# Attention values in one group of matmuls per key block instead of two half groups

## The chip, the cores and the metric

The kernel runs on one core of a Trainium2 chip. The metric is the device time of one execution in microseconds; the kernel before has a median of 934.62 us in three runs.

## The reference

Two transformer layers on 2048 tokens of width 128. The change touches the first layer's attention alone, which has 8 heads, 2 query and key dimensions and 16 value dimensions a head, over all 2048 keys:

```python
q = (x @ Wq.T + bq).reshape(B, M, H, dqk)      # dqk = 2
k = (x @ Wk.T + bk).reshape(B, M, H, dqk)
v = (x @ Wv.T + bv).reshape(B, M, H, dv)       # dv = 16
scores = einsum('bmhd,bnhd->bhmn', q, k) / sqrt(dqk)
scores = where(scores >= 0, scores, 0.2 * scores)
beta = softmax(scores, axis=-1)
out = gamma * einsum('bhmn,bnhd->bmhd', beta, v) + x
...
```

Around it stand a mixture of 64 experts with 6 chosen, a lookup attention and a mixture of 8 experts with 2 chosen, each behind a layer norm. They are the same in both kernels.

## The kernel before

The attention stage works in 8 rounds: 4 chunks of 512 queries (`c`) times 2 groups of 4 heads (`g`). A round goes over 16 key blocks of 128 keys (`n`), and a key block is two pairs (`hp` 0 and 1), a pair being two heads. So there are 256 pairs, numbered `u`, 32 in a round; an even `u` is the first pair of its key block, an odd one the second. The keys lie on the partitions of the scores and the queries in the columns.

A pair goes through these steps, each on 128 partitions by 2 x 512 columns:
- `scores(u)` on PE (line 575): two bf16 products, side by side in the array, into two banks of PSUM. There are three such buffers of two banks, used in turn, so scores(u) waits until exp(u-3) has read them (`exp_done`).
- relu, `max(4 s, 0)` in place, on DVE (line 1474). In the rounds with the routing work (below), slots 14, 25, 27 and 31 are on ACT instead (line 1011).
- `shifted(u)` on PE (line 588): two bf16 products that add the scores once more, less a bound per query, onto the same banks. It waits for the relu.
- exp on ACT (line 1015) into a float32 buffer `PB` in SBUF, which holds a whole key block. There are three, and exp of a block's first pair waits until the values of three blocks ago are done (`values_done`).
- `values(u)` on PE (line 603): the exps times the values `VS`, 32 columns a head (16 values, a one for the sum, zeros). The four heads of the group have a quarter of the array's columns each, and add up over the 16 key blocks in one bank of PSUM, 6 or 7 by the round. A float32 product shows as two records in the trace. Each group covers all four heads and half of the queries, so it needs both exps of its block.

PE's order is written out by hand: for each u, shifted(u), then scores(u+2), then values(u-2). After the fifth exp of a round ACT copies the sums of the round before out of PSUM (line 994). In the three rounds with c >= 1 and g = 0, the norm and the router of the chunk before are done in between: PE's parts stand behind the values of slots 6, 9 (line 617), 18 (626), 21 (633) and 28 (642 to 648) of the 32, DVE's behind slots 8, 11, 13, 24, 26 and 30. The scatter of the chunk's rows by POOL (line 1197) is paced by counts of exps; that of the last chunk follows the stage.

Of the kernel before, what the change touches and what calls it, by code (L numbers as in the profile page):

```python
# [14 lines left out]
NT = T // P  # L15
BANK = 512
CH = 512
# [4 lines left out]
HG = H // G  # L22
# [101 lines left out]
def build(nc, a, out):  # L124
# [12 lines left out]
    with ctx:  # L137
        def sb(name, shape, dt=f32, stack=ctx):
            return stack.enter_context(nc.sbuf_tensor(name, shape, dt))
# [3 lines left out]
        def sem(name):  # L143
            if name not in sems:
                sems[name] = ctx.enter_context(nc.semaphore(name))
            return sems[name]
# [36 lines left out]
        PS = ctx.enter_context(nc.psum_tensor("PS", [P, 8 * BANK], f32))  # L183
# [5 lines left out]
        def cb(name, lo=0, hi=None):  # L189
            s, e = BC[name]  # L190
            return CB[:, s + lo:(s + hi if hi else e)]

        def pf(name):
            s, e = PFC[name]
            return PF[:, s:e]
# [34 lines left out]
        PB = [sb(f"PB{i}", [P, HG, CH], f32, att) for i in range(3)]  # L230
# [3 lines left out]
        VS = sb("VS", [P, NT, H, 32], f32, att)  # L234
# [85 lines left out]
        def pair_of(u):  # L320

            rnd, r = divmod(u, PER_ROUND)
            c, g = ROUNDS[rnd]
            return rnd, c, g, r // 2, r % 2
# [141 lines left out]
        def _(pe):  # L466
            mm = nc.tensor.matmul
# [68 lines left out]
            for g in range(G):  # L536
                mm(PS[:, g * P:(g + 1) * P], hxy[:, g, 0, :], pf("vx"), start=True, stop=False)
                last = mm(PS[:, g * P:(g + 1) * P], hxy[:, g, 1, :], pf("vy"), start=False, stop=True)
# [6 lines left out]
            for i in range(4):  # L545
                if i >= 2:
                    pe.wait_ge(sem("bound_ready"), i - 1)
                for t in range(4 * i, 4 * i + 4):
                    for g in range(G):
                        at = 2 * (i % 2) * BANK + (2 * (t % 4) + g) * P  # L550
                        last = mm(PS[:, at:at + P], QS[g][:, t * P:(t + 1) * P], VV[:, g * P:(g + 1) * P], start=True, stop=True)
# [8 lines left out]
            for g in range(G):  # L560
                for t in range(NT):
                    last = mm(PS[:, 4 * g * BANK + t * P:4 * g * BANK + (t + 1) * P], MR[:, g, t, :], cb("identb"), start=(g == 0),
                              stop=True, skip_group_check=True)
# [27 lines left out]

            def values(u):

                rnd, c, g, n, part = pair_of(u)
                if n == 0 and part == 0 and rnd >= 2:
                    pe.wait_ge(sem("sums_taken"), rnd - 1)
                    if g == 1:
                        pe.wait_ge(sem("counts0_out"), c)
                pe.wait_ge(sem("exp_done"), u - part + 2)
                q = slice(part * CH // 2, (part + 1) * CH // 2)  # L600
                at = (6 + rnd % 2) * BANK
                for j in range(HG):
                    last = mm(PS[32 * j:32 * j + 32, at + q.start:at + q.stop], VS[:, n, g * HG + j, :],  # L603
                              PB[u // 2 % 3][:, 2 * (j % 2) + j // 2, q], start=(n == 0 and part == 0), stop=(n == NT - 1),
                              skip_group_check=True)
                last.then_inc(sem("values_done"), 1)

            def sums_turned(q, part, b):

# [44 lines left out]
            for u in range(N_PAIRS):  # L654
                shifted(u)
                if u + 2 < N_PAIRS:
                    scores(u + 2)
                if u >= 2:
                    values(u - 2)
                rnd, c, g, n, hp = pair_of(u)  # L660
                r = u % PER_ROUND
                if c >= 1 and g == 0:
                    if r == 6:
                        sums_turned(c - 1, 0, 7)
                    if r == 9:
                        sums_turned(c - 1, 1, 7)
                    if r == 18:
                        rows_turned(c - 1, 7)
                    if r == 21:
                        gates0(c - 1, 7)  # L670
                    if r == 28:
                        counts0(c - 1, 7)
            values(N_PAIRS - 2)
            values(N_PAIRS - 1)

            pe.wait_ge(sem("counts0_out"), NC - 1)
# [33 lines left out]
            for k in range(2):  # L710
                for h in range(2):
                    last = mm(PS[0:1, 2 * BANK + (2 * k + h) * P:2 * BANK + (2 * k + h + 1) * P], tcol[:, k, h:h + 1], ident,
                              start=True, stop=True)
# [1155 lines left out]
```

## Time and profile before

| | |
|---|---|
| median of 3 runs | 934.62 us (931.69 to 935.87) |
| the profiled execution | 936.18 us, of which span 934.4 us |
| PE busy | 715.6 us, 77% of the span |
| DVE busy | 630.0 us, 67% |
| ACT busy | 449.1 us, 48% |
| mean granted clock of TensorE | 0.863 |

Busy times are shares of the whole span, which has many stages. The attention stage runs from about 52 to 382 us. PE here is TensorE's matmul, PEld its weight loads, DVE VectorE, ACT ScalarE, POOL GpSimd, SP SyncE. In the groups, "L603" is line 603. The ends of matmuls are modelled, so their starts are the better measure. In the chain a step counts up to the start of the next one, so the records of a group overlap less there than in the timeline.

### The profile page before, as it was taken

Reading aid. Unit: us, or ns where it says so; the run is one execution under the profiler, and the core shown is the slowest. Engines: PE = TensorE matmul, PEld = TensorE weight load, DVE = VectorE, ACT = ScalarE, POOL = GpSimd, SP = SyncE. Lnnn points to the kernel's source line nnn. Section 1 sums busy time; section 2 is a strip of 40 time slices with the busy share of each in tenths; the row PEclk is TensorE's granted clock in tenths of the full one; section 3 lists DMA queues with packets and bytes.
Section 4 is the critical chain, followed back from the end, with each engine's and each line's share of the span. In section 5 each row is a group of like instructions: output and inputs, shape, how many; then the busy total and the mean of one; then the engine's idle time right before and its main releaser. Section 6 shows DMA issues by size and latency. Waiting matters only on the chain.

```text
span 934.4 us, 17256 instructions
## 1 busy us (share of the span) xinstructions
PE 715.6 (77%) x5879; PEld 424.4 (45%) x5880; DVE 630.0 (67%) x1367; ACT 449.1 (48%) x605; POOL 432.6 (46%) x671
## 2 busy tenths in 40 slices
PE   4789999999999999538898998016264653699992
PEld 2332223223222222214898998013223422699992
DVE  7879998999899999373576754246767454244442
ACT  3668887888888888301343444001101011365550
POOL 5010002362254235455676775677657552255552
PEclk9879999999999999869899999556575556799997
DMA  4499999999999901512697665112111110143336
GB/s 156 144 270 276 302 282 312 362 290 298 288 303 314 297 22 44 127 51 75 179 259 221 166 172 146 45 50 52 51 45 49 44 43 24 37 51 48 48 49 149
DMA packets 83334, 143.45 MB, mean 154 GB/s; under 512 B 10720, under 2 KB 75584, under 8 KB 81744
## 3 DMA queue, kind: packets, MB, share of 16 engines
q1 hardware_dynamic: 57600, 118.07, 43.5%
q0 software_dynamic: 12784, 17.40, 8.3%
q10 hardware_dynamic: 12864, 6.89, 2.6%
q8 instruction: 48, 0.79, 0.4%
q14 instruction: 38, 0.31, 0.1%
HBM read 117.13 MB, written 101.34 MB: 234 GB/s over the span
## 4 chain that ended last, share of the span: by engine, by line
PE 59%; DVE 12%; POOL 8%; DMA 7%; issue 6%; ACT 6%; SPq 2%; POOLq 0%; DVEq 0%
PE PS L603 13%; PE PS L588 7%; PE PS L575 7%; PE PS L907 6%; ACT PB L1015 3%; PE PS L751 3%; POOL GB L1239 3%; DMA XP<-slots_scratch 3%; PE PS L917 3%; PE PS L738 3%; PE PS L740 3%; POOL slots_scratch L1197 2%; PE PS L726 2%; PE PS L855 1%; DMA sums_scratch<-YO,XG 1%
## 5 line engine op out<-in xcount | busy, mean ns | idle before, releaser
L1474 DVE TENSOR_SCALAR PS<-PS 128x1024 f32<-128x1024 f32 x244 | 289.7, 1227 | 15.5 <-PE PS L575 11.6
L1015 ACT ACTIVATE PB<-PS 128x1024 f32<-128x1024 f32 x256 | 260.5, 1025 | 54.3 <-PE PS L588 46.6
L603 PE MATMUL PS<-PB,VS 128*32 128x256 f32 x2048 | 164.2, 393 | 0.6 <-ACT PB L1015 0.5
L1197 POOL DMA_INDIRECT slots_scratch<-XN,slot x96 | 93.6, 975 | 59.8 <-ACT PB L1015 39.0
L1239 POOL DMA_INDIRECT GB<-y_scratch,slotc x96 | 91.7, 955 | 37.0 <-issue 28.6
L575 PE MATMUL PS<-QS,KP 64*128 64x512 bf16 x512 | 99.3, 385 | 10.7 <-ACT PB L1015 6.0
L588 PE MATMUL PS<-QM,KP 64*128 64x512 bf16 x512 | 100.7, 390 | 1.3 <-DVE PS L1474 1.2
L1282 POOL DMA_INDIRECT sums_scratch<-YO,XG x39 | 60.8, 1558 | 61.9 <-DVE YO L1797 58.8
L907 PE MATMUL PS<-XTT,WB 128*128 128x128 f32 x624 | 78.4, 281 | 0.0
L907 PEld LDWEIGHTS PS<-XTT,WB 128*128 128x128 f32 x624 | 75.0, 197 | 0.3 <-issue 0.3
L588 PEld LDWEIGHTS PS<-QM,KP 64*128 64x128 bf16 x512 | 24.6, 93 | 104.3 <-issue 50.4
L603 PEld LDWEIGHTS PS<-PB,VS 128*32 128x32 f32 x2048 | 40.5, 108 | 65.6 <-issue 64.1
L1074 ACT COPY XT<-PS 128x512 f32<-128x512 f32 x8 | 4.7, 585 | 122.9 <-PE PS L775 122.9
L1223 POOL COPY WQ<-W0GU 128x192 f32 x160 | 55.3, 346 | 14.8 <-issue 10.4
L1207 POOL TENSOR_TENSOR X<-X,TQ 128x256 f32<-128x256 f32 x8 | 5.8, 724 | 121.3 <-DVE TQ L1425 121.3
L775 PE MATMUL PS<-CF,XN 128*128 128x128 f32 x32 | 8.9, 434 | 68.8 <-DVE XN L1617 68.8
L1790 DVE COPY XTT<-PS 128x128 f32<-128x128 f32 x39 | 11.4, 291 | 70.8 <-PE PS L895 70.8
L1604 DVE SCALAR_TENSOR_TENSOR X<-GB,wtok,X 128x128 f32<-128x128 f32 x96 | 33.7, 352 | 31.2 <-DMA GB<-y_scratch,slotc 28.4
L575 PEld LDWEIGHTS PS<-QS,KP 64*128 64x128 bf16 x512 | 24.5, 93 | 60.5 <-ACT PB L1015 47.8
L1063 ACT ACTIVATE SP<-PS 96x256 f32<-96x256 f32 x80 | 30.4, 380 | 45.0 <-PE PS L740 44.8
L1116 ACT COPY WB<-W1GU 128x1024 f32 x39 | 40.7, 1046 | 22.7 <-PE PS L907 15.0
L1040 ACT COPY YP<-PS 128x256 f32<-128x256 f32 x80 | 29.8, 372 | 40.1 <-PE PS L751 39.9
(281 smaller groups left out, 1298.5 us busy)
## 6 DMA issues: line engine op xcount, KB each, us to landing
y_scratch<-YP SPq DMA_DIRECT2D x80, 128.0 KB, 2.5
slots_scratch<-slots_scratch SPq DMA_DIRECT2D x1, 8768.0 KB, 37.1
W0GU<-in_w0gu SPq DMA_DIRECT2D x1, 6144.0 KB, 124.3
XP<-slots_scratch ACTq DMA_DIRECT2D x80, 64.0 KB, 2.7
XP<-slots_scratch SPq DMA_DIRECT2D x80, 64.0 KB, 2.7
W1GU<-in_w1gu SPq DMA_DIRECT2D x8, 512.0 KB, 4.3
W0D<-in_w0d SPq DMA_DIRECT2D x1, 3072.0 KB, 16.7
XG<-slots_scratch SPq DMA_DIRECT2D x39, 68.5 KB, 2.2
```

Source lines behind the costliest of these rows:

```text
L575: last = mm(bank(2 * (u % 3) + k), KP[g][hp][r, n * P:(n + 1) * P], QS[g][r, c * CH:(c + 1) * CH], start=True, stop=True)
L588: last = mm(bank(2 * (u % 3) + k), KP[g][hp][r, n * P:(n + 1) * P], QM[g][r, c * CH:(c + 1) * CH], start=False, stop=True, skip_group_chec ...
L603: last = mm(PS[32 * j:32 * j + 32, at + q.start:at + q.stop], VS[:, n, g * HG + j, :], PB[u // 2 % 3][:, 2 * (j % 2) + j // 2, q], start=( ...
L907: last = mm(PS[:, at + k * P:at + (k + 1) * P], WB[j % 2][:, w], XTT[j % 2][:, :], start=True, stop=True)
L1015: A(PB[u // 2 % 3][:, 2 * hp:2 * hp + 2, :], pair_banks(u).rearrange("p (j q) -> p j q", j=2), ACT.Exp).then_inc(sem("exp_done"), 1)
L1116: nc.scalar.copy(WB[j % 2][:, :], W1GU[:, ds(expert, 1), :].squeeze(1)).then_inc(sem("w_placed"), 1)
L1197: gp.indirect_dma_start(slots0_dram.rearrange("b p d -> (b p) d"), bass.IndirectOffsetOnAxis(ap=slot0[:, t, k:k + 1], axis=0), XN[:, t, 0: ...
L1223: gp.tensor_copy(WQ[j % 6][:, :], W0GU[:, ds(expert, 1), :].squeeze(1)).then_inc(sem("wq_ready"), 1)
L1239: gp.indirect_dma_start(GB[:, t, k, :], None, y0_dram.rearrange("b p d -> (b p) d"), bass.IndirectOffsetOnAxis(ap=slotc[:, t, k:k + 1], ax ...
L1282: gp.indirect_dma_start(sums_dram[j % 2][:, :], bass.IndirectOffsetOnAxis(ap=XG[j % NXG][:, P:P + 1].bitcast(i32), axis=0), YO[j % 4][:, : ...
L1474: TS_(pair_banks(u), pair_banks(u), 4.0, 0.0, ALU.mult, ALU.max).then_inc(sem("relu_done"), 1)
L1604: step(STT(X[:, t, :], GB[:, t, k, :], wtok[:, t, k:k + 1], X[:, t, :], ALU.mult, ALU.add))
```

## The change

The values products of a key block run once, for all 512 queries, behind the second pair (odd u) of the block in PE's order; behind the first pair nothing is left. The count `values_done` goes up by 2 there instead of by 1 twice. Types, operands and the accumulation over key blocks stay.

```diff
--- before.py
+++ after.py
@@ -591,19 +591,18 @@
 
             def values(u):
 
-                rnd, c, g, n, part = pair_of(u)
-                if n == 0 and part == 0 and rnd >= 2:
+                rnd, c, g, n, hp = pair_of(u)
+                if hp == 0:
+                    return
+                if n == 0 and rnd >= 2:
                     pe.wait_ge(sem("sums_taken"), rnd - 1)
                     if g == 1:
                         pe.wait_ge(sem("counts0_out"), c)
-                pe.wait_ge(sem("exp_done"), u - part + 2)
-                q = slice(part * CH // 2, (part + 1) * CH // 2)
-                at = (6 + rnd % 2) * BANK
+                pe.wait_ge(sem("exp_done"), u + 1)
                 for j in range(HG):
-                    last = mm(PS[32 * j:32 * j + 32, at + q.start:at + q.stop], VS[:, n, g * HG + j, :],
-                              PB[u // 2 % 3][:, 2 * (j % 2) + j // 2, q], start=(n == 0 and part == 0), stop=(n == NT - 1),
-                              skip_group_check=True)
-                last.then_inc(sem("values_done"), 1)
+                    last = mm(PS[32 * j:32 * j + 32, (6 + rnd % 2) * BANK:(7 + rnd % 2) * BANK], VS[:, n, g * HG + j, :],
+                              PB[u // 2 % 3][:, 2 * (j % 2) + j // 2, :], start=(n == 0), stop=(n == NT - 1), skip_group_check=True)
+                last.then_inc(sem("values_done"), 2)
 
             def sums_turned(q, part, b):
```

## Rows read from the trace of the kernel before

**Rows 1.** The page: busy times, and the span in 40 slices of 23.4 us.

```profile
PE 715.6 (77%) x5879; PEld 424.4 (45%) x5880; DVE 630.0 (67%) x1367; ACT 449.1 (48%) x605; POOL 432.6 (46%) x671
...
PE   4789999999999999538898998016264653699992
...
DVE  7879998999899999373576754246767454244442
...
PEclk9879999999999999869899999556575556799997
DMA  4499999999999901512697665112111110143336
```

**Rows 2.** The page: costliest groups (busy us, mean ns | idle before, releaser).

```profile
L1474 DVE TENSOR_SCALAR PS<-PS 128x1024 f32<-128x1024 f32 x244 | 289.7, 1227 | 15.5 <-PE PS L575 11.6
L1015 ACT ACTIVATE PB<-PS 128x1024 f32<-128x1024 f32 x256 | 260.5, 1025 | 54.3 <-PE PS L588 46.6
L603 PE MATMUL PS<-PB,VS 128*32 128x256 f32 x2048 | 164.2, 393 | 0.6 <-ACT PB L1015 0.5
...
L575 PE MATMUL PS<-QS,KP 64*128 64x512 bf16 x512 | 99.3, 385 | 10.7 <-ACT PB L1015 6.0
L588 PE MATMUL PS<-QM,KP 64*128 64x512 bf16 x512 | 100.7, 390 | 1.3 <-DVE PS L1474 1.2
```

**Rows 3.** Timeline of ACT, copies of the sums: start us, us.

```profile
100.18 0.58 ACT L994 COPY OT<-PS 128x512 f32<-128x512 f32 x1
...
138.72 0.58 ACT L994 COPY OT<-PS 128x512 f32<-128x512 f32 x1
...
182.96 0.58 ACT L994 COPY OT<-PS 128x512 f32<-128x512 f32 x1
```

**Rows 4.** The chain in a plain stretch: start us, us, what.

```profile
120.96 0.39 PE PS L575 x2
121.34 0.57 PE PS L603 x8
121.91 0.32 PE PS L588 x2
122.24 0.22 PE PS L575 x2
122.45 0.57 PE PS L603 x8
123.02 0.32 PE PS L588 x2
```

**Rows 5.** Timeline of PE, same stretch.

```profile
120.96 0.39 PE L575 MATMUL PS<-QS,KP 64*128 64x512 bf16 x2
121.28 0.64 PE L603 MATMUL PS<-PB,VS 128*32 128x256 f32 x8
121.85 0.39 PE L588 MATMUL PS<-QM,KP 64*128 64x512 bf16 x2
122.07 0.38 PE L575 MATMUL PS<-QS,KP 64*128 64x512 bf16 x2
...
123.36 0.39 PE L575 MATMUL PS<-QS,KP 64*128 64x512 bf16 x2
```

**Rows 6.** Timeline of ACT, same stretch.

```profile
120.98 1.02 ACT L1015 ACTIVATE PB<-PS 128x1024 f32<-128x1024 f32 x1
122.28 1.02 ACT L1015 ACTIVATE PB<-PS 128x1024 f32<-128x1024 f32 x1 [0.27 <-PE PS L588]
```

**Rows 7.** Timeline of DVE, three relus that start one after the other.

```profile
120.13 2.49 DVE L1474 TENSOR_SCALAR PS<-PS 128x1024 f32<-128x1024 f32 x2
...
121.39 1.23 DVE L1474 TENSOR_SCALAR PS<-PS 128x1024 f32<-128x1024 f32 x1
...
122.53 1.22 DVE L1474 TENSOR_SCALAR PS<-PS 128x1024 f32<-128x1024 f32 x1
```

**Rows 8.** Windows of 2.40 us and lulls: busy by engine, granted clock.

```profile
core 0: us, PE busy (x) PEld busy (x) DVE busy (x) ACT busy (x) POOL busy (x), PEclk, DMA share, GB/s
...
119.98:122.38 2.40, 2.39 (x26) 0.69 (x24) 2.36 (x3) 2.04 (x3) 0.00 (x0) 1.00 0.48 137
...
164.00:170.00 6.00, 5.13 (x50) 1.32 (x48) 5.83 (x19) 6.00 (x9) 0.72 (x1) 1.00 1.04 445
460.00:467.00 7.00, 4.27 (x24) 4.27 (x25) 2.03 (x6) 1.25 (x4) 1.57 (x7) 0.76 0.62 156
500.00:511.00 11.00, 8.85 (x67) 8.63 (x66) 5.69 (x15) 3.38 (x9) 5.66 (x19) 0.84 0.72 201
```

**Rows 9.** The values line: ns min, median, max.

```profile
L603 PE MATMUL PS<-PB,VS x2048: 378/403/634, 57.5 to 381.7; 128*32 128x256 f32 x187
```

**Rows 10.** Line 695, float32 records of 512 columns; its timeline.

```profile
L695 PE MATMUL PS<-XT,wshg x32: 591/592/1169, 412.4 to 436.9; 128*96 128x512 f32 x32
...
421.24 3.60 PE L695 MATMUL PS<-XT,wshg 128*96 128x512 f32 x8
```

**Rows 11.** The chain in a mixed round: routing pieces on PE.

```profile
141.24 0.59 PE PS L617 x4
...
157.39 0.59 PE PS L626 x4
...
161.78 1.03 PE PS L633 x8
...
172.13 0.21 PE PS L642
172.34 0.17 PE PS L645 x3
172.51 0.11 PE PS L648
```

**Rows 12.** The chain at the stage's end.

```profile
380.99 1.11 PE PS L603 x16
```

**Rows 13.** Timeline of PE at the lower clock.

```profile
56.93 0.61 PE L575 MATMUL PS<-QS,KP 64*128 64x512 bf16 x2
57.47 1.08 PE L603 MATMUL PS<-PB,VS 128*32 128x256 f32 x8
58.48 0.61 PE L588 MATMUL PS<-QM,KP 64*128 64x512 bf16 x2
```

## Prediction

> **What bounds the kernel now.** I read the page first, for its busy times and its forty slices. PE, DVE and ACT are all busy through the first dense stretch, and PE and DVE both read as full there [rows 1]. That stretch is the attention stage, and the three costliest lines of the kernel lie in it [rows 2]. A busy share near 100% on two engines doesn't say which one sets the pace, so I went on to the order of time.
>
> The copies of the finished sums stand at the same place in every round and so mark the rounds [rows 3]. A round without the routing work (plain) takes 100.18 to 138.72, or 38.54 us for 32 pairs: 1.20 us a pair. A round with it (mixed) takes 138.72 to 182.96, or 44.24 us. There are five plain rounds and three mixed ones.
>
> The chain of a plain stretch is PE alone, in a pattern that repeats after two pairs and 2.40 us [rows 4]. But the chain hides that two of its steps only just made it. The timeline shows this [rows 5, 6]. With the starts there:
> - exp (ACT) of a pair starts at 120.98, takes 1.02, ends at 122.00, and the scores that need its banks run from 122.07. In the other half of the pattern it is 122.28 + 1.02 = 123.30, and the scores start at 123.36: they waited for exp.
> - From those scores to the values products behind them: 120.96 to 121.28, 0.32 us.
> - From the values products to the shifted scores behind them: 121.28 to 121.85, 0.57 us.
> - From the shifted scores to the exp that they release: 121.85 to 122.28, 0.43 us, and the exp takes 1.02 + 0.06 to the next scores.
>
> These make a closed loop: exp(u-1), scores(u+2), values(u-2), shifted(u+1), exp(u+1). The scores wait for exp because there are three buffers of pair banks, and PE works in program order. Its length is 1.02 + 0.06 + 0.32 + 0.57 + 0.43 = 2.40 us for two pairs, exactly the measured pattern. DVE is next: its starts are 120.13, 121.39, 122.53 [rows 7], so 1.26 us apart where it waits for scores and 1.14 where it has work. DVE alone could do two pairs in 2.28. ACT does its two in 2.04 [rows 8].
>
> **The change, part by part.** Removed: per key block, eight matmul records (four products, two records each) of 256 columns, and their eight weight loads. Added: the remaining eight have 512 columns. Moved: all of a block's values work stands behind the odd pair; behind the even pair there is nothing. No DMA is moved.
>
> *The length of the wide group.* A 256-column record takes 378 ns at the least (median 403) [rows 9]. The trace has no products of 32 stationary columns by 512, but it has float32 records of 512 columns, and those take 591 ns at the least and follow each other every (3.60 - 0.59) / 7 = 0.43 us [rows 10]. So 512 columns cost 0.213 us more in each of the two passes of a group; the four heads run side by side in both cases. Group: 0.57 + 2 x 0.213 = 1.00 us. Lower bound: the passes alone, 2 x 0.43 = 0.86. Upper bound: nothing saved over two narrow groups, 1.14. I take 1.00, since the same chip clock and the same type stand in the row.
>
> A page of the Trainium skill, TensorEngine Tiling (Array Packing), section Instruction Overhead, says that each matmul carries about 60 cycles of overhead. By it, as an estimate, dropping eight records in two pairs would save 8 x 25 ns = 0.20 us of the 1.14, and the group would be 0.94 us; the loop below would be 2.77 us instead of 2.83, some 8 us less in all. No row here separates the overhead of a record, since four run at once.
>
> *What it frees.* PE work in two pairs falls from 2 x 0.57 to 1.00, so by 0.14 us. That is worth something only if PE's total work is the limit.
>
> *What it lengthens.* The loop through the odd pair now holds the wide group: 1.02 + 0.06 + 0.32 + 1.00 + 0.43 = 2.83 us for two pairs. The loop through the even pair has no values group: about 1.02 + 0.06 + 0.22 + 0.43 = 1.73 (0.22 is scores right behind shifted [rows 4]). A loop can't be averaged with the other, since each comes round once in two pairs, and the longer one sets the pace. So a plain pair goes from 1.20 to 1.415 us, +0.213. Followed in time from an exp of an even pair at 0: the next exp, whose shifted scores were ready long before, runs 1.02 to 2.04; the scores wait until 1.08; the wide group runs 1.40 to 2.40; the shifted scores of the next even pair, whose relu was ready, only then start, and its exp at 2.83. DVE has relus for 2.28 of each 2.83 and waits; ACT for 2.04.
>
> *The waits.* values(u-2) needs the exps of its whole block, that is up to u-2. At that point PE has already waited for exp(u-1) in the scores ahead of it, so no new wait arises. The buffers of exp's output are freed at the same slot as before for the odd pair, and exp of three blocks later is behind shifted scores that stand behind that group; no wait there. The sums of a round are complete at the same slot.
>
> *Mixed rounds.* A mixed round costs 44.24 - 38.54 = 5.7 us over a plain one. PE's inserted work is 0.59 + 0.59 + 0.59 + 1.03 + 0.21 + 0.17 + 0.11 = 3.29 us [rows 11] (the piece of line 617 comes twice and stands there once); the rest, 2.4, is ACT and DVE work, among it four relus on ACT. After the change the pieces behind even pairs (slots 6, 18, 28) fall into the short loop, which has 2.83 - 1.73 = 1.1 us to spare, and cost nothing. Slots 9 and 21 are odd and add 0.59 + 1.03 = 1.62 to the long loop. Of the 2.4 on ACT and DVE, something between all and none remains, since ACT's spare time in two pairs grows from 0.36 to 0.79. Surcharge: 1.6 to 4.0, I take 2.8. A mixed round becomes 32 x 1.415 + 2.8 = 48.1 us, +3.8.
>
> *Behind the stage.* The work after the last exp is a chain of its own [rows 12]: it shortens by about 0.1 (two narrow groups, 1.11, become one of 1.00). POOL's scatters inside the stage wait for counts of exps and stretch with it; its last 24 come after. The background transfers end before the stage does [rows 1] and gain slack.
>
> **Sum.** Five plain rounds x 32 x 0.213 = 34.1, less about 0.6 because the first pairs run at the start-up and the last ones drain: 33.5. Three mixed rounds x 3.8 = 11.4. Together +45. The profiled execution took 936.2 us (span 934.4 and 1.8 around it), 1.6 above the median of the three runs shown. 936.2 + 45 - 1.6 = 979.6; I say 979 us, 4.8% slower.
>
> **The rivals.**
> - *The pace follows PE's total work (same or a little better).* If the two loops were averaged, or the buffers gave enough slack, two pairs would need DVE's 2.28. Then plain pairs gain 0.06 us, 160 x 0.06 = 9.6 us, and mixed ones perhaps half: 921 to 926 us. For it: DVE is 98% busy [rows 8], and in the average over two pairs every engine has room. Against it: the loop of five measured steps gives the measured 2.40 to the last digit, and none of its waits is loosened by the change. With enough slack in the buffers to absorb just the lump but no more, it would be 935.
> - *The wide group costs no more than a narrow one (faster, the other side).* If a group's 0.57 were a price per instruction and not per column, V = 0.57, PE would be free for longer and the loop would stay at 2.40; mixed rounds would get up to 2 us shorter each: about 929. It decides at V = 0.57: every 0.01 above costs 0.005 x 256 = 1.3 us. Against it: [rows 9, 10], 378 against 591 ns.
> - *The clock.* PE now has holes of up to 0.7 us in 2.83 us. The granted clock fell where PE sat idle for microseconds at a stretch, to a mean of 0.76 and 0.84, and stayed at 1.00 in the lull of a mixed round [rows 8]. At the lower level (1.2 GHz) a narrow group takes 57.47 to 58.48, 1.01 us, scores to values 0.54, shifted scores 0.61 [rows 13]. The loop would be 1.08 + 0.54 + (1.01 + 0.85) + 0.66 = 4.14, +0.65 us a pair on top; with a fifth of the stage at that level, 979 + 33 = 1012.
> - *The group is dearer than two narrow ones make it look* (V = 1.14): loop 2.97, 1.485 a pair. Plain 160 x 0.285 = 45.6, mixed 3 x 6.1 = 18: 998 us. With V = 0.86: loop 2.69, plain 160 x 0.145 = 23.2, mixed 3 x 1.6 = 4.8: 962.
>
> **How the numbers follow.** Forecast (slower by the long loop, group of 0.86 to 1.14): 0.87. Clock on top of it: 0.04. Pace by total work: 0.06, of which half within 0.5% of before. Group at the narrow price: 0.03. A measurement of this kernel tells about 0.5% from no change, 4.7 us. Slower 0.91, same 0.03, faster 0.06. The range comes from the group's length, mostly between 0.88 and 1.10, and the mixed surcharge between 1.6 and 5.7 us (-3.6 to +8.7 in all): 964 to 993. It leaves out the clock and both faster rivals.
>
> **What would show it.** In the profile after, 1024 records of L603 (its new line) with 512 columns near 0.59 us; the chain of a plain stretch as exp, scores, values 1.00, shifted, with exp pairs every 2.83 us; rounds near 45.3 and 48 us between the copies; ACT and DVE with their busy times unchanged and their idle time before exp and relu grown by some 40 us, released by PE; a granted clock of 1.00. A group near 0.57, or rounds of 38 us, would make the prediction wrong; so would rounds of 45 with a gap elsewhere given back, of which I see none.

## The result and the profile after

The changed kernel takes 972.34 us (971.05 to 974.88, 4 runs) against 933.62 us for the one before in the same session: ratio 1.042, interval 1.038 to 1.045. It is slower by 39 us. (The profile after has one source line fewer, so that exp is line 1014 and relu 1473.) The profiled execution took 974.88 us, 38.7 more than that of before (936.18). The forecast was 979 us, range 964 to 993.

The page of the profile after, its busy times and slices; it answers to [rows 1]:

```profile
PE 682.4 (70%) x4855; PEld 392.8 (40%) x4856; DVE 639.9 (66%) x1367; ACT 440.0 (45%) x605; POOL 432.3 (44%) x671
...
PE   4777777877877787744888999403653654499992
...
DVE  7788888888888889837366774236677564144442
...
PEclk9889999999999999986999999855756557699996
```

PE has 1024 records fewer and 33 us less to do, and the stage is longer. In its slices PE reads 7 where it read 9, DVE 8 where it read 9, and the granted clock reads 9 from the fourth slice on until the stage ends, as it did before. No engine is full any more, which points to waits and not to work. The costliest groups answer to [rows 2]:

```profile
L1473 DVE TENSOR_SCALAR PS<-PS 128x1024 f32<-128x1024 f32 x244 | 299.1, 1232 | 45.4 <-PE PS L575 38.1
L1014 ACT ACTIVATE PB<-PS 128x1024 f32<-128x1024 f32 x256 | 250.7, 1022 | 104.6 <-PE PS L588 103.9
L575 PE MATMUL PS<-QS,KP 64*128 64x512 bf16 x512 | 99.3, 385 | 78.8 <-ACT PB L1014 76.1
L603 PE MATMUL PS<-PB,VS 128*32 128x512 f32 x1024 | 137.1, 608 | 0.6 <-ACT PB L1014 0.6
```

The idle time before exp went from 54.3 to 104.6 us and ends with the shifted scores; that before relu from 15.5 to 45.4, ended by the scores; that before the scores from 10.7 to 78.8, ended by exp. These three waits point at each other in a ring. The chain in a plain stretch shows the ring, and answers to [rows 4]:

```profile
131.28 1.03 ACT PB L1014
132.32 0.05 issue
132.36 0.39 PE PS L575 x2
132.75 0.99 PE PS L603 x8
133.75 0.34 PE PS L588 x2
134.09 0.02 issue
134.11 1.03 ACT PB L1014
```

exp at 131.28, scores at 132.36, wide values group, shifted scores, exp at 134.11: 2.83 us for two pairs, to the last digit of the forecast. The timeline of PE gives the starts, and answers to [rows 5]:

```profile
132.36 0.39 PE L575 MATMUL PS<-QS,KP 64*128 64x512 bf16 x2 [0.69 <-ACT PB L1014]
132.68 1.06 PE L603 MATMUL PS<-PB,VS 128*32 128x512 f32 x8
133.68 0.39 PE L588 MATMUL PS<-QM,KP 64*128 64x512 bf16 x2
```

132.68 to 133.68 is the group: 1.00 us. Ahead of it PE sits idle for 0.69 us, waiting for exp; behind it everything waits for PE. The copies of the sums answer to [rows 3]:

```profile
106.75 0.58 ACT L993 COPY OT<-PS 128x512 f32<-128x512 f32 x1
...
152.00 0.58 ACT L993 COPY OT<-PS 128x512 f32<-128x512 f32 x1
...
199.16 0.58 ACT L993 COPY OT<-PS 128x512 f32<-128x512 f32 x1
```

A plain round takes 152.00 - 106.75 = 45.25 us (38.54 before), a mixed one 47.16 (44.24 before). The stage ends, by its last copy, at 422.9 us instead of 382.1: +40.8. Some 2 us come back behind it: the stage of the 64 experts (first to last turned pair) took 133.1 instead of 136.2 us, in single executions.

### The profile page after: what moved, and what is told of

The parts are those of the page before. It is cut to its first block, busy times and chain, and to the rows that moved or that the text cites. A ratio compares the mean times of both kernels' runs of the same rounds, so it can differ in the third digit from the quotient of the medians.

```text
span 973.1 us, 15208 instructions
## 1 busy us (share of the span) xinstructions
PE 682.4 (70%) x4855; PEld 392.8 (40%) x4856; DVE 639.9 (66%) x1367; ACT 440.0 (45%) x605; POOL 432.3 (44%) x671
## 4 chain that ended last, share of the span: by engine, by line
PE 52%; ACT 16%; DVE 13%; DMA 7%; POOL 6%; issue 5%; SPq 2%; POOLq 0%; DVEq 0%
ACT PB L1014 13%; PE PS L603 12%; PE PS L906 7%; PE PS L575 5%; PE PS L588 4%; DMA XP<-slots_scratch 4%; PE PS L916 3%; POOL GB L1238 3%; PE PS L750 3%; PE PS L737 2%; PE PS L739 2%; PE PS L725 1%; PE PS L854 1%; ACT PS L1010 1%; DMA sums_scratch<-YO,XG 1%
## 5 line engine op out<-in xcount | busy, mean ns | idle before, releaser
L1473 DVE TENSOR_SCALAR PS<-PS 128x1024 f32<-128x1024 f32 x244 | 299.1, 1232 | 45.4 <-PE PS L575 38.1
L1014 ACT ACTIVATE PB<-PS 128x1024 f32<-128x1024 f32 x256 | 250.7, 1022 | 104.6 <-PE PS L588 103.9
L575 PE MATMUL PS<-QS,KP 64*128 64x512 bf16 x512 | 99.3, 385 | 78.8 <-ACT PB L1014 76.1
L603 PE MATMUL PS<-PB,VS 128*32 128x512 f32 x1024 | 137.1, 608 | 0.6 <-ACT PB L1014 0.6
L1549 DVE COPY XQ<-PS 128x256 f32<-128x256 f32 x54 | 22.9, 425 | 33.3 <-PE PS L725 33.3
```

The costliest lines, as they stand in the source:

```text
L575: last = mm(bank(2 * (u % 3) + k), KP[g][hp][r, n * P:(n + 1) * P], QS[g][r, c * CH:(c + 1) * CH], start=True, stop=True)
L603: last = mm(PS[32 * j:32 * j + 32, (6 + rnd % 2) * BANK:(7 + rnd % 2) * BANK], VS[:, n, g * HG + j, :], PB[u // 2 % 3][:, 2 * (j % 2) + j ...
L1014: A(PB[u // 2 % 3][:, 2 * hp:2 * hp + 2, :], pair_banks(u).rearrange("p (j q) -> p j q", j=2), ACT.Exp).then_inc(sem("exp_done"), 1)
L1473: TS_(pair_banks(u), pair_banks(u), 4.0, 0.0, ALU.mult, ALU.max).then_inc(sem("relu_done"), 1)
```

## The experiments

The experiments ran on three chips: the first four on one, the repeats and the two bf16 kernels on a second, and the other four, in a single execution each, on a third. On the first two of these chips the stages behind attention were 53 to 59 us longer, for every kernel profiled there, than in the first profile of the kernel before, which itself took 1016 and 1003 us there. So the totals that were expected in us can't be compared with the measured ones. I read ratios, and above all the rounds inside the stage, which no later stage touches: 45.25 us for the changed kernel in its first profile and again on the second chip.

**Two narrow groups together.** Is it the wide product, or the place of the work?

```diff
-                for j in range(HG):
-                    last = mm(PS[... whole bank ...], VS[:, n, g * HG + j, :], PB[...][:, 2 * (j % 2) + j // 2, :], ...)
+                for part in range(2):
+                    q = slice(part * CH // 2, (part + 1) * CH // 2)
+                    for j in range(HG):
+                        last = mm(PS[... half bank q ...], VS[:, n, g * HG + j, :], PB[...][:, 2 * (j % 2) + j // 2, q], ...)
```

> The changed kernel, but the block's values products are two narrow groups (256 queries each) one right after the other behind the odd pair, instead of one wide group. Theory (the loop exp, scores, values, shifted, exp through the odd pair sets the pace, with the length of all the values work that stands in it): the lump is 1.11 to 1.14 us instead of 1.00, two pairs take 2.94 to 2.97 us instead of 2.83, a plain round 47.0 to 47.5 us, the kernel 986 to 990 us, though PE's total work is just that of the kernel before. Rival (the wide product itself is what costs, not the place): two narrow groups are as before, 2.40 us for two pairs and about 934 us.

Ratio 1.022 to the kernel before on its chip (interval 1.017 to 1.027, so it is slower, though not clearly by 2%), and a plain round of 152.76 - 107.43 = 45.33 us in the first of them. Its chain:

```profile
120.67 1.03 ACT PB L1018
121.70 0.05 issue
121.75 0.39 PE PS L575 x2
122.14 1.00 PE PS L606 x16
123.14 0.34 PE PS L588 x2
123.48 0.02 issue
123.51 1.03 ACT PB L1018
```

It is the place: narrow products in the lump are as slow as wide ones, with 2.84 us for two pairs, though PE issues exactly the records of the kernel before. The size was expected too long: 16 narrow records take 1.00 us, not 1.11 to 1.14. So a second narrow group right behind the first adds only 0.43 us, and of a lone group's 0.57 us, 0.14 is paid once for the whole run of values products, however many records it has. The ratio is smaller than the rounds make one expect: no profile of the kernel before was taken on this chip, but on the second one its attention stage was itself longer, as told below.

**Half the queries, and three quarters.** Does the lump's length set the pace even when PE has far less to do?

```diff
-                    last = mm(PS[32 * j:32 * j + 32, (6 + rnd % 2) * BANK:(7 + rnd % 2) * BANK], VS[:, n, g * HG + j, :],
-                              PB[u // 2 % 3][:, 2 * (j % 2) + j // 2, :], ...)
+                    w = CH if n == 0 else CH // 2          # 384 and 32 in the two others
+                    last = mm(PS[32 * j:32 * j + 32, at:at + w], VS[:, n, g * HG + j, :],
+                              PB[u // 2 % 3][:, 2 * (j % 2) + j // 2, 0:w], ...)
```

> The changed kernel, with the values products of key blocks 1 to 15 of a round only for the first 256 queries (the other half of these products is left out), behind the odd pair. Theory: the group is as long as a narrow one, 0.57 us, so the long loop is 1.83 + 0.57 = 2.40 us for two pairs, the same as in the kernel before, although half of the values work is gone and nothing stands behind the even pairs; plain rounds near 38.6 us, mixed ones some 41 to 42, in all about 920 to 926 us. Rival (the pace follows an engine's total work, DVE's 1.14 us a pair being the next): 2.28 us for two pairs, plain rounds near 36.6 us, about 912 us.

> The changed kernel, with the values products of key blocks 1 to 15 only for the first 384 queries (a quarter of these products is left out). Theory: the group takes 1.00 - 2 x 0.107 = 0.79 us, the long loop 2.62 us for two pairs, a plain round 41.9 us: on the line between 38.85 (256 queries) and 45.25 (512). Rival (the pace has steps, or follows total work): anything off that line.

Copies of the sums with half the queries, then with 384:

```profile
98.47 0.58 ACT L995 COPY OT<-PS 128x512 f32<-128x512 f32 x1
...
137.33 0.58 ACT L995 COPY OT<-PS 128x512 f32<-128x512 f32 x1
```

```profile
102.31 0.58 ACT L995 COPY OT<-PS 128x512 f32<-128x512 f32 x1
...
144.36 0.58 ACT L995 COPY OT<-PS 128x512 f32<-128x512 f32 x1
```

Plain rounds of 38.86 and 42.05 us. With half of the values work left out, a plain round is no shorter than in the kernel before (38.54), as the loop of 1.83 + 0.57 = 2.40 says and total work denies. The first key block of a round keeps its full group, so the round is 15 x 2.40 + 2.83 = 38.83 us. The three points 256, 384 and 512 queries lie on a line, 38.86, 42.05 and 45.25: 3.2 us a step over the 15 shortened blocks, or 0.213 us a block for each 128 queries, which is the forecast's price of streaming. The mixed round with half the queries took 42.9 us, more than the 41 to 42 expected. Its ratio is 0.974 (0.969 to 0.979), more of a gain than its stage shows (last copy at 376.7 us, 382.1 in the first profile of the kernel before); some of that may be the late exps told below, but the kernel before was not profiled on this chip. The one run with 384 took 957.7 us beside 936.6.

**Nearly no values.**

> The changed kernel, with the values products of key blocks 1 to 15 only for 32 queries (nearly all of these products are left out). Theory: the group takes some 0.2 us, the long loop 2.05 us, below DVE's two relus of 2.28 us, so the line ends there: a plain round 36.3 to 36.8 us as in the bf16 kernels, not the 33 us that the loop alone would give. Rival (PE alone sets the pace in float32): below 36 us.

Windows of that kernel, the plain rounds 1, 3 and 5 (the columns are those of [rows 8]):

```profile
95.10:132.30 37.20, 28.91 (x256) 8.68 (x256) 36.76 (x33) 32.89 (x34) 0.00 (x0) 0.95 0.99 283
...
178.30:216.60 38.30, 31.98 (x256) 9.00 (x256) 37.70 (x33) 32.85 (x35) 19.14 (x20) 0.82 1.00 296
261.60:298.50 36.90, 28.03 (x256) 8.57 (x256) 36.53 (x33) 32.93 (x34) 19.13 (x20) 1.00 0.98 299
```

A partial miss: 36.9 us at full clock, 37.2 and 38.3 where the granted clock fell to its lower level for part of the round. DVE is busy for 36.5 of 36.9 us, so the line does end at DVE. The whole took 931.3 us beside 936.6. What I hadn't counted on is that the granted clock falls inside the stage when PE has this little left to do. In the changed kernel it did not.

**Values ahead of the scores.** The same wide group, moved out of the loop of exp.

```diff
                 shifted(u)
-                if u + 2 < N_PAIRS:
-                    scores(u + 2)
                 if u >= 2:
                     values(u - 2)
+                if u + 2 < N_PAIRS:
+                    scores(u + 2)
```

> The changed kernel, with PE's order shifted(u), values(u-2), scores(u+2) instead of shifted, scores, values. Theory: the wide group leaves the loop of exp (which becomes 1.73 us) but enters the one of relu: relu 1.23, to shifted 0.05, to values 0.32, to scores 1.00, to relu 0.44, which is 3.04 us for two pairs instead of 2.83; plain rounds near 48.6 us and the kernel near 995 to 1000 us. Rival (only the loop through exp counts, or PE's hole before the scores swallows the group): 2.28 to 2.4 us for two pairs and the kernel at or below the kernel before, 915 to 935 us.

Ratio 1.043 (1.038 to 1.048). Its chain has DVE where ACT was:

```profile
120.07 1.24 DVE PS L1473
...
121.36 0.39 PE PS L588 x2
121.75 0.99 PE PS L603 x8
122.75 0.34 PE PS L575 x2
...
123.11 1.24 DVE PS L1473
```

3.04 us for two pairs and a plain round of 157.69 - 109.05 = 48.64 us, both as expected. The hole of 0.69 us ahead of the scores can't be filled this way: the group then delays the scores, and through them relu. Both rings run through PE, and in both of the places tried one of them holds the lump.

**The routing pieces on even slots.**

```diff
-                    if r == 9:
+                    if r == 10:
                         sums_turned(c - 1, 1, 7)
...
-                    if r == 21:
+                    if r == 22:
                         gates0(c - 1, 7)
```

> The changed kernel, with the two routing pieces of PE that stand behind wide groups (slots 9 and 21, 0.59 and 1.03 us) moved one slot on, to 10 and 22, where no values group stands. Theory: there they lie in the short loop, which has 1.1 us to spare, and a mixed round (47.15 us, 1.9 over a plain one) loses up to 1.6 us: 45.5 to 46.2 us, the kernel 3 to 5 us faster than the changed one. Rival (the surcharge is ACT's and DVE's work, or the later release of ACT makes it good): mixed rounds stay at 47 us and the time doesn't move.

The mixed round between its copies went from 47.16 to 198.30 - 152.01 = 46.29 us, just outside the range expected: 0.87 us of the 1.62. The stage ends at 420.35 us, 2.6 earlier. Its ratio on the chip of the first four is 1.016 (1.013 to 1.020); that session has no run of the changed kernel to set it against. Its chain at slot 10 shows what takes the place:

```profile
159.75 0.60 PE PS L616 x4
160.35 0.02 issue
160.38 0.27 DVE og L1423
160.65 0.02 issue
160.67 0.48 DVE TQ L1424
161.15 1.15 DVE PS L1473
```

PE had room for the piece there, but DVE waits for its result right behind slot 11, and now stands waiting with the next relu behind it. This leaves 0.37 us. At slot 22 it is ACT that reads the piece's result (line 1003) ahead of a relu and the next exps, and 0.61 us are left. I had counted PE's room and not the distance to the reader.

**Products in one pass.** The group shortened with nothing left out: exp's output and the values are rounded to bf16.

```diff
-        PB = [sb(f"PB{i}", [P, HG, CH], f32, att) for i in range(3)]
+        PB = [sb(f"PB{i}", [P, HG, CH], bf16, att) for i in range(3)]
...
-        VS = sb("VS", [P, NT, H, 32], f32, att)
+        VS = sb("VS", [P, NT, H, 32], bf16, att)
```

> The changed kernel, with exp's output and the values in bf16 instead of float32 (the sums are still added in float32), so that a product is one pass and not two. Theory: the wide group takes 0.21 + 0.14 = 0.35 us, the long loop 2.18 us, which is below DVE's two relus of 2.28, so DVE sets the pace: plain rounds near 36.6 us, mixed ones 41 to 42, and the kernel faster than the one before by some 18 to 22 us in the stage. Lumping costs nothing once the group is under 0.45 us. Rival (the order of PE costs 0.2 us a pair whatever the length): plain rounds of 40 us or more.

> The kernel before (two narrow groups), with exp's output and the values in bf16. Theory: narrow group 0.25 us, loops 2.08 us, DVE sets the pace at 2.28: the same stage time as the wide bf16 kernel within 1 us a round. Rival (fewer, wider instructions help once PE is not in the loop): the wide one is faster by its 0.14 us a key block, 2 us a round.

Copies of the sums, wide and then narrow:

```profile
94.49 0.58 ACT L993 COPY OT<-PS 128x512 f32<-128x512 f32 x1
...
130.80 0.58 ACT L993 COPY OT<-PS 128x512 f32<-128x512 f32 x1
```

```profile
96.31 0.58 ACT L994 COPY OT<-PS 128x512 f32<-128x512 f32 x1
...
132.62 0.58 ACT L994 COPY OT<-PS 128x512 f32<-128x512 f32 x1
```

Both plain rounds take 36.31 us: by the sum, a group under 2.28 - 1.83 = 0.45 us leaves the bound to DVE, and lumping is free. Where nothing held the products behind a group, the wide one took 0.33 us and the narrow one 0.22, start to start. A wide one:

```profile
58.57 0.39 PE L575 MATMUL PS<-QS,KP 64*128 64x512 bf16 x2 [0.41 <-ACT PB L1014]
58.89 0.40 PE L603 MATMUL PS<-PB,VS 128*32 128x512 bf16 x4
59.22 0.39 PE L588 MATMUL PS<-QM,KP 64*128 64x512 bf16 x2
```

The difference, 0.11 us, is 256 columns, so 512 columns stream in 0.21 us, a quarter of the 0.86 in float32 (half as many records, each half as long). 0.12 us is left over in either group, though every product around it is bf16 too. So most of the 0.14 us of the float32 group is not the price of a change of type. The products also change their shape in the array there, from 64x128 to 128x32 and back; no run separates that from other causes.

Against the kernel before, the wide one has a ratio of 0.969 (0.966 to 0.972), the narrow one 0.975 (0.973 to 0.977). Both beat both kernels of this study. Of the 7 us between the two medians, 3.9 lie in the stage of the profiled executions. There the later plain rounds, in which scatters run, are 36.7 and 36.5 us in the wide one against 38.0 and 37.9 in the narrow one, more than the 1 us a round that was expected. In each of those rounds of the narrow one a single exp starts 1.3 to 1.4 us late, with ACT free and the shifted scores there (at 178.32 and 258.07 us), which is as much as the two kernels differ; so it is not the groups that cost the time. Two of three mixed rounds go the other way by 0.9 us (42.7 in the wide one, outside the 41 to 42 expected); at the end of both, the wide one's granted clock fell to the lower level (238.8 to 242.2 and 317.3 to 324.1 us).

**The two kernels again, on the second chip.**

> The kernel before, unchanged, as a control for this chip, whose stages behind attention ran some 50 us longer in the first four experiments. Expected: plain rounds 38.54 us and mixed ones 44.25 us, as in the first profile, a ratio of 1, and the extra time in the stages behind attention. If the rounds differ here, the experiments have to be read against them.

> The changed kernel, unchanged, on the same chip. Expected: plain rounds 45.25 us and mixed ones 47.15 us, the last copy of the sums 40.8 us later than in the kernel before. If the ratio is again 1.042 the loss is the stage's; if it is nearer 1.02, as the first four experiments suggest, some 20 us are given back in the stages behind it on this chip, and the two traces show where.

Ratio of the first 1.001 (0.998 to 1.003), of the changed kernel 1.028 (1.025 to 1.031). The difference to 1.042 does not lie behind the stage, as was expected, but in the stage, and in the kernel before. Its round 3, which in the first profile took 38.54 us:

```profile
183.75 0.58 ACT L994 COPY OT<-PS 128x512 f32<-128x512 f32 x1
...
224.69 0.58 ACT L994 COPY OT<-PS 128x512 f32<-128x512 f32 x1
```

40.94 us here, and rounds 5 and 7 grew too, so that its stage ends at 395.2 instead of 382.1. The changed kernel's rounds are 45.25 and 47.15 on this chip as well, and its stage ends at 422.6. Its loss in the stage is thus 27.4 us here and 40.8 there. The timeline of ACT and PE in that round shows a late exp:

```profile
204.34 2.16 ACT L1015 ACTIVATE PB<-PS 128x1024 f32<-128x1024 f32 x2 [0.28 <-issue]
...
206.31 0.39 PE L588 MATMUL PS<-QM,KP 64*128 64x512 bf16 x2
...
207.44 1.94 ACT L1015 ACTIVATE PB<-PS 128x1024 f32<-128x1024 f32 x2 [0.94 <-PE PS L588]
```

ACT is free at 206.50 and the shifted scores of 206.31 release exp 0.43 us later, at 206.74 as everywhere else; it starts at 207.44, 0.7 us late. In rounds 5 and 7 this comes about every fourth pair. Over the three rounds the late starts add up to some 13 us, as much as the stage is longer.

**What makes exp late?**

```diff
                 chunk_norm(q)
                 chunk_route(q)
+            for q in range(NC):
                 chunk_scatter(q)
```

> The kernel before, unchanged, as the control of this call: plain rounds 38.54 us where no scatters run, and either 38.5 or 39 to 43 us in the plain rounds with scatters, by the chip.

> The kernel before, with POOL's 72 scatters of the first three chunks moved behind the attention stage. It is for the late starts of exp (0.7 us every fourth pair) that the kernel before showed in the rounds with scatters on the second chip. If the scatters' transfers cause them, all plain rounds here are 38.54 us, also where the control of this call has more; if not, they stay long. The whole gets some 90 us longer in any case (72 scatters at 1.26 us).

Inconclusive. This chip behaved as the first one: in one execution the control took 936.8 us with all plain rounds at 38.54, and so did the kernel with the scatters behind the stage (1025.1 us in all). With nothing to remove, the run says nothing on the cause.

## Why the prediction was right

- *What bounds the kernel.* Right: the loop exp, scores, values, shifted, exp. The group's length moves the pace by just its own length (256, 384, 512 queries), the same records in another place cost the same as the wide ones, and where the group leaves this loop it enters the one of relu with the length worked out for it.
- *The wide group.* 1.00 us forecast, 1.00 measured. The upper bound of 1.14 counted twice what is paid once: two narrow groups in a row take 1.00 too. By the rule of about 60 cycles for each matmul (the Trainium skill, TensorEngine Tiling (Array Packing), Instruction Overhead), read as a cost that every record adds, the wide group would have been shorter than two narrow ones in a row by eight records' worth, 0.20 us as an estimate; the trace doesn't agree: 45.25 against 45.33 us a round is 0.005 us a key block. Why the extra records cost nothing, no run shows.
- *Plain rounds.* +6.8 us forecast, +6.71 measured.
- *Mixed rounds.* The term that was mis-sized: a surcharge of 2.8 us (1.6 to 4.0), where 1.90 was measured, so +2.9 a round instead of +3.8, and 2.7 us in all. The two pieces behind wide groups cost their full 1.62 us, as they stand in the chain with the whole of their length:

```profile
159.20 0.59 PE PS L616 x4
...
176.76 1.03 PE PS L632 x8
```

From exp to exp, those two steps are 0.58 and 1.04 us over 2.83, and the pieces behind even pairs cost nothing, as forecast. Of the 2.4 us of ACT and DVE work only 0.28 remains, where 1.2 was taken. That ACT's longer waits take in the rest is likely but was not tested by itself.
- *Sum.* The stage grew by 40.8 us, not 45: 2.7 of the difference is the mixed rounds; 1.4 is the plain ones, of which the first and the last grew less than I took (6.6 up to the first copy, 5.4 behind the seventh, 3 x 6.71 between). The 0.1 us saved at the end did not come: the last group takes 1.11 up to the copy of the sums, as the two before it did.
- *Behind the stage.* Nothing was forecast to come back; 2.1 us did in the profiled pair of executions. Its cause was not looked for. The forecast of 979 us was 7 too high; 4.2 of that is the stage and 2.1 this.
- *The rivals.* Total work as the pace is refuted by the kernel with half the queries; the price per instruction by 1.00 against 0.57; the granted clock was 1.00 from 60 us to the end of the stage, in both kernels. It fell inside the stage with 32 queries and, for 3 to 7 us at a time, in both bf16 kernels.

What stays open is why the kernel before loses 13 us in the stage on the second chip, through exps that start 0.7 us late in the rounds with scatters, and why the changed kernel shows none of it. That a late start hides in ACT's idle time, 0.8 us ahead of each two exps, is only argued, and the kernel with two narrow groups together speaks against it: it has the same idle time, and its rounds 3 and 5 grew to 46.3 and 46.5 us all the same, with two exps each 0.5 to 0.6 us late. Late exps showed only in three kernels, all with two narrow groups a key block (the one before on the second chip, the one with both groups together, the narrow bf16 one); the kernel with half the queries, with one narrow group a block, ran on the same chip as the second of them and had none. They make the changed kernel's loss 28 us instead of 39 there, with the same sign.

No run changed the number of buffers of the scores. That link of the ring rests on the traced waits of the scores for exp.

## What to carry to other kernels

Where a few buffers tie engines into a ring, add the ring up by starts, from one wait to the same wait, and compare it with the busiest engine's work: an in-order engine's lump of work that sits in it costs its full length, even while that engine's total work falls and none of them is full. Two half-size groups in alternate slots beat one full group as long as the ring with the lump is longer than the next bound; once the lump is short (here under 0.45 us by the sum, and 0.33 in the run that shows it), the split buys nothing. When work is moved into an engine's spare time, look at who reads its result and how soon.

## What the hardware showed beside that

- Products of 32 stationary columns, four side by side, between products of another shape: in float32 0.43 us for 256 columns and 0.86 for 512, in bf16 0.11 and 0.21, plus 0.14 us (0.12 in bf16) once around the run of them. Sixteen float32 records took no longer than eight of twice the length.
- PE's granted clock fell to its lower level inside the stage when only 32 queries' values were left (0.95 and 0.82 as means of rounds), while the matmul records still covered 28.9 of 37.2 us; at 34.2 of 45.2 us, in the changed kernel, it stayed at 1.00. Ahead of the fall at 99.5 us PE had stood idle for no longer than 0.56 us at a time since 94 us.
- Chips differ in more than a scale: the same kernel took 934 us in the first session, 937 on one chip and 1003 and 1016 on two others. Of the 68 us between the first profile and that of 1005 us, 36 lie in the stage in which POOL gathers rows by index (line 1239, first to last 136.6 and 172.6 us) and 13 in attention. A ratio of two kernels moved from 1.042 to 1.028.
